# Third attention of a fused four-layer kernel: the row maxima of two heads in one reduction, with the PSUM banks shared out anew

## The reference, cut to what matters

```
qkv = einsum('bnd,ed->bne', z, W_qkv); q, kk, v = 16 heads of 8 channels each
scores = einsum('bhnd,bhmd->bhnm', q, kk) * scale
A = softmax(scores, axis=-1)            # all 512 x 512 scores of a head, no mask
out = einsum('bhnm,bhmd->bhnd', A, v)
x = x + out
```

## Time and profile before

| | us |
|---|---|
| median of three runs | 2079.42 |
| the profiled execution's own time | 2071.99 |
| its span (first to last instruction) | 2070.1 |
| TensorE busy | 1803.5 (87%) |
| VectorE busy | 1292.1 (62%) |
| ScalarE busy | 1042.6 (50%) |
| mean granted TensorE clock | 0.937 |

### The profile page before, as it was taken

The page is one execution under the profiler, slowest core; times in us unless marked ns, Lnnn a source line. Parts: engine busy times, 40 slices in busy tenths (PEclk is TensorE's granted clock), DMA queues, the critical chain, the costliest instruction groups (busy, mean ns, idle before and its releaser), DMA issues.

```text
span 2070.1 us, 33125 instructions
## 1 busy us (share of the span) xinstructions
PE 1803.5 (87%) x11885; PEld 811.1 (39%) x11885; DVE 1292.1 (62%) x3442; ACT 1042.6 (50%) x1768; POOL 713.1 (34%) x796
## 2 busy tenths in 40 slices
PE   4888888656559999998999999999999957999998
PEld 1233333234424444444445443233333234444443
DVE  3777777367767777771111114999999537766663
ACT  1566666412116666663223221888888834454432
POOL 4476776535442223201011012222223036444420
PEclk9899999768869999998999998999999969999999
DMA  5453222000024322400000010333222010000000
GB/s 132 114 139 80 62 67 58 1 17 1 0 61 107 80 63 64 113 11 3 0 0 1 0 49 13 85 88 76 63 63 62 2 51 1 6 6 6 6 11 11
DMA packets 67963, 91.68 MB, mean 44 GB/s; under 512 B 10924, under 2 KB 61340, under 8 KB 62924
## 3 DMA queue, kind: packets, MB, share of 16 engines
q1 hardware_dynamic: 66072, 89.04, 18.1%
q10 hardware_dynamic: 1728, 0.53, 0.2%
HBM read 49.30 MB, written 39.85 MB: 43 GB/s over the span
## 4 chain that ended last, share of the span: by engine, by line
PE 52%; issue 5%; DVE 3%; ACT 3%; DMA 2%; SPq 1%; POOL 1%; DVEq 0%; ACTq 0%; POOLq 0%
PE ps L1442 5%; PE ps L412 5%; PE ps L1454 5%; PE ps L386 4%; PE ps L2885 3%; PE ps L1419 3%; PE ps L2155 3%; PE ps L398 3%; PE ps L2157 2%; PE ps L2173 2%; PE ps L370 2%; PE ps L332 2%; DMA Qst<-mT 2%; PE ps L354 1%; PE ps L1848 1%
## 5 line engine op out<-in xcount | busy, mean ns | idle before, releaser
L702 DVE TENSOR_REDUCE mx<-ps 128x1 f32<-128x512 f32 (+3 forms) x1024 | 534.1, 582 | 108.3 <-PE ps L354 80.0
L600 ACT ACTIVATE Pr<-ps 128x1024 f32<-128x1024 f32 (+3 forms) x512 | 348.0, 706 | 179.3 <-PE ps L337 92.3
L593 ACT ACTIVATE Pr<-ps 128x512 f32<-128x512 f32 x512 | 275.3, 601 | 44.2 <-PE ps L386 37.4
L354 PE MATMUL ps<-Kst,Qst 63*128 63x512 bf16 (+3 forms) x1024 | 221.9, 315 | 55.2 <-DVE mx L702 29.4
L698 DVE CUSTOM_DVE_ANT_0 vs<-ps,cT 128x512 f32<-128x512 f32 (+3 forms) x512 | 225.8, 488 | 61.5 <-PE ps L354 58.0
L332 PE MATMUL ps<-Qst,Kst 64*128 64x512 bf16 (+3 forms) x1024 | 221.8, 310 | 16.9 <-ACT Pr L600 8.4
L2913 POOL TENSOR_TENSOR ve<-mv,eps 128x4 f32<-128x4 f32 x41 | 8.8, 215 | 577.3 <-DVE mv L2902 577.3
L370 PE MATMUL ps<-Pr,V 128*32 128x512 f32 (+3 forms) x2048 | 198.3, 460 | 6.4 <-ACT ctxU L606 2.9
L398 PE MATMUL ps<-Kst,Qst 63*128 63x512 bf16 x512 | 172.7, 404 | 5.5 <-DVE mx L702 3.3
L412 PE MATMUL ps<-Pr,V 128*32 128x256 f32 x2048 | 164.5, 393 | 8.5 <-ACT ctxU L606 7.6
L386 PE MATMUL ps<-Qst,Kst 64*128 64x512 bf16 x512 | 157.6, 388 | 9.7 <-DMA Qst<-mT 5.7
(11 more groups left out here) (340 smaller groups left out, 3272.1 us busy)
## 6 DMA issues: line engine op xcount, KB each, us to landing
Qst<-parts_scratch SPq DMA_DIRECT2D x48, 384.0 KB, 6.4
Kst<-parts_scratch SPq DMA_DIRECT2D x48, 384.0 KB, 8.4
parts_scratch<-qpart SPq DMA_DIRECT2D x24, 384.0 KB, 2.7
parts_scratch<-kpart SPq DMA_DIRECT2D x24, 384.0 KB, 3.2
parts_scratch<-qpart SPq DMA_DIRECT2D x24, 256.0 KB, 2.9
parts_scratch<-kpart SPq DMA_DIRECT2D x24, 256.0 KB, 3.3
parts_scratch<-qpart SPq DMA_DIRECT2D x24, 128.0 KB, 2.8
parts_scratch<-kpart SPq DMA_DIRECT2D x24, 128.0 KB, 3.3
```

The lines of the kernel that those rows point to most:

```text
L354: mm = pe.matmul(ps[:, 4 + a, lo:lo + W], k.Qst[rows, n.par, pair, P * it:P * it + P], k.Kst[rows, n.par, pair, 0:W], start=True, stop=True)
L593: act.activation(k.Pr[:, g % 2, 2 * (j // 2) + 1 - j % 2, :], ps[:, self.bank_t(b, g, j), :], ACT.Exp).then_inc(self.s_exp.sem, 1)
L600: act.activation(k.Pr[:, g % 2, 2 * tile:2 * tile + 2, 0:W], ps[:, 2 * tile:2 * tile + 2, 0:W], ACT.Exp).then_inc(self.s_exp.sem, 1)
L702: dve.tensor_reduce(k.mx[:, half, at:at + 1], ps[:, bank, lo:lo + W], AX_X, ALU.max, negate=True).then_inc(self.s_max.sem, 1)
```

## The change

Row scores get four banks (2 to 5) in two pairs, transposed scores two banks (0 and 1). The two M tiles of a pair of heads go into two neighbouring banks, and one reduction on VectorE over 128 x 2 x 512 takes both maxima. On TensorE the order becomes T0 M0 M1 T1 PV T2 M2 M3 T3 PV. T now waits for the exponential two tiles back, M for the pair two pairs back.

```diff
     def bank_t(self, b, g, j):
-        return (64 * b.c + 4 * g + j) % 3
-
-    def bank_m(self, n, u):
-        return 3 + (64 * n.c + u) % 3
+        return j % 2
+
+    def banks_m(self, u):
+        return 2 + 2 * (u // 2 % 2)
@@ head_t
-            pe.wait_ge(self.s_exp.sem, self.s_exp.at(b, 4 * g + j - 2))
+            pe.wait_ge(self.s_exp.sem, self.s_exp.at(b, 4 * g + j - 1))
@@ head_m
-            pe.wait_ge(self.s_max.sem, self.s_max.at(n, u - 2))
-            pe.matmul(ps[:, self.bank_m(n, u), :], k.Qst[rows, n.par, pair, P * it:P * it + P],
+            pe.wait_ge(self.s_max.sem, self.s_max.at(n, u - a - 2))
+            pe.matmul(ps[:, self.banks_m(u) + a, :], k.Qst[rows, n.par, pair, P * it:P * it + P],
@@ frame of TensorE
-                        if mb.valid():
+                        if mb.valid() and j in (0, 2):
                             head_m(mb, c, j)
+                            head_m(mb, c, j + 1)
@@ maxima
+            if self.kind == "full":
+                for _, u, (it,) in fills[0::2]:
+                    dve.wait_ge(self.s_scores.sem, self.s_scores.at(n, u + 2))
+                    if u % 32 == 0:
+
+                        dve.wait_ge(self.s_mT_ps.sem, self.s_mT_ps.at(n.plus(-1), half + 1))
+                    at = self.banks_m(u)
+                    dve.tensor_reduce(k.mx[:, half, :].rearrange("p (a r) -> p a r", a=2)[:, :, 4 * i + it],
+                                      ps[:, at:at + 2, :], AX_X, ALU.max, negate=True).then_inc(self.s_max.sem, 2)
+                return
```

More of the change, by code:

```diff
@@ L693, in maxima @@
                     at = 16 * a + 4 * i + it
-                    bank = self.bank_m(n, u) if self.kind == "full" else 4 + a
+                    bank = 4 + a
                     if self.kind == "alibi":
```

## The result

The changed kernel takes 2096.41 us in the median of four runs (2094.38 to 2098.70), the kernel before 2077.31 us in runs beside it. The ratio is 1.0098, 95% interval 1.0082 to 1.0113: slower by 0.98%, which is 19 to 20 us. The forecast was 2096 us, in a range of 2080 to 2108.

What follows compares the result with a forecast made beforehand. TensorE was taken to set the pace, busy 43 to 44 us per frame. 7.5 frames x (2.8 - 0.7) = 15.8, -1.1 at the start and +2.5 at the end, made +17.2 on 2079.4: forecast 2096 us, range 2080 to 2108.

Steps and rivals of the forecast that it cites:

- The step that carried it: In a slot with both tile kinds, T3 waits for T1's exponential: a stall of 0.23 us, slot 2.45 instead of 2.22.
- the pair's length: VectorE's reduction over two banks, 1024 elements instead of 512, was to last 1.22 us.
- pitch: Time between starts of back-to-back pair reductions on VectorE: 1.14 us against 1.20 for two single ones.
- the start: Ten slots of row scores alone at VectorE's pace: twenty pairs take 22.8 us instead of 23.9, -1.1 us.
- the last batch: End of the stage, eight slots with T alone at 2.45 instead of 2.08 us: 3.0 us, taken as 2.5.
- The frame's sum: Per frame of 16 slots, stalls of 2.8 us less VectorE's 0.7 us; a frame should take 47.5 us.
- The charge for the stalls: Per frame, 16 stalls of T3, four hidden in waits for the copy of bank 6: 12 x 0.23 = 2.8 us.
- VectorE's relief: Wide reductions save VectorE 1.9 us per frame, of which TensorE was credited with 0.7 us.
- The ceiling of 1.8 us per frame: Most that VectorE's saving could give TensorE: M's waits in weight load and matmul, (8.9 + 2.1) / 6.
- A hidden stall: Rival: T's stalls fall into existing waits and VectorE's gain counts, -6 to -15 us, say 2070 us; chance 0.10.
- cancelling: Rival: stalls cost 2.8 us a frame, VectorE's relief gives the full 1.8; +9 us, 2088 us; chance 0.15.
- a slow reduction: Rival: a two-bank reduction costs two without overlap, 1.36 us, and VectorE becomes the bound; 2115 us; chance 0.05.

Runs made afterwards that it cites:

- the wait alone: Kernel before with T waiting for the exponential two tiles back instead of three, banks, order and reductions as before: 2099.82 us, ratio 1.0105.
- the short copy of V: Changed kernel with ScalarE's copy of V after slot 10 over 128 of 512 columns in the third attention: 2097.72 us in one execution.
- unpaired: Changed kernel with each pair's maxima taken by two reductions of 512 instead of one of 1024: 2097.83 us, ratio 1.0094 against the kernel before.
- the shorter maxima: Kernel before with maxima over 480 of 512 columns in the third attention: 2072.20 us, ratio 0.9978.
- the best: Kernel before with order T0 M0 M1 T1, the transpose of the maxima left between M2 and M3: 2077.01 us, ratio 0.9996.

## Why the prediction was right, and where it was not

**Right in cause and size.** The step that carried it, T3 waits for the exponential of T1 and starts at T0 + 1.57 instead of 1.34, was met to 0.02 us in the slots where ScalarE is free, and the wait alone reproduces the loss. The other terms with a row of their own were met nearly or wholly: the pair's length (1.22 us forecast, 1.221 measured) and pitch (1.14, 1.133), the start (-1.1, measured -0.84) and the last batch (half a frame at 2.1 plus 2.5, 3.6; measured 3.6). Seven frames at +2.1 make 14.7; measured 15.6. The stage was to get 17.2 us longer and got 18.3. That the total was met to 0.4 us is in part luck: the 17.2 us were added to a median of 2079.42 us, which with one more run became 2077.31.

**The frame's sum came near because its errors offset each other.** It was +2.1 us; measured +2.35 (47.72 - 45.37). The charge for the stalls was 12 x 0.23 = 2.8 us. The wait alone measured 2.5 (47.86 - 45.37). By slots:

- 0, 2, 8, 10 and 12 pay 0.2 as worked out (0.16 to 0.23).
- 9 and 13 hide the stall in the wait for bank 6 (-0.02 and +0.08). In slot 5, the fourth of this kind, there is no such wait to hide in: the waits for the copy are 18 in six frames, three a frame and not four, and slot 5 pays 0.41. Slot 1 gets 0.24 shorter, for VectorE is what is late there, and the stall of slot 0 gives it time.
- 6 and 14 pay nothing: the transpose of the maxima stands between T2 and T3 there and holds T3 until 1.65 us in the kernel before. The prediction had every projection and transpose at the end of a slot. 7 and 15 pay nothing because they end in the wait for the landing row, which the prediction had left to the range.
- 3, 4, 5 and 11 pay 0.40. I had taken the 0.43 us from T0 to the exponential from one slot, in which ScalarE was free; behind a copy it is 0.60, and the short copy of V showed that this is the cause in slot 11.

**VectorE's relief was given to the wrong part of the change.** The 0.7 us per frame that I credited to the wide reduction is worth nothing there (unpaired: every slot the same), and 0.25 us even with three T banks. What gave time back is the fourth M bank: slot 1 fell from 3.79 to 3.24 us. I had called this part free of cost and given it no gain. From it 0.42 us go off again for the transpose behind M3, for which the prediction had no term. The ceiling of 1.8 us per frame from the waits was far too high as a price: 8.9 of its 11.0 us stood at a weight load, where the shorter maxima show that a wait is mostly free: 1.9 us less work gave 0.25.

**What a merge saves, and what a bank is worth.** By an estimate from the Trainium skill's fixed 120 cycles ("VectorE: DVE Perf Modes", the TRN2 errata section) a merge would have saved 0.125 us per pair; measured are 1.196 - 1.133 = 0.063 us, and the measurement decides. The Trainium skill's advice to rotate independent matmul groups through banks ("Perfetto Trace Analysis", Optimizing Tensor Performance, Matmuls) bears on both sides here. This case's traces agree with it: T lost a bank and 2.5 us per frame, M won one and 0.55 us in slot 1.

**The rivals.** A hidden stall is refuted by T3's start; cancelling by the frames; a slow reduction by its pitch. What I said would show in the waits came only in part: T (L386) waits for the exponential at its weight load, 81.8 us in six frames against 58.2 before, but hardly as idle time of PE, for M covers it. VectorE's busy time was to fall to 40 us and fell to 41.3: a reduction that waits for its M is counted in full, where back to back ones overlap. ScalarE's was to stay at 38 us and is 39.1.

**Two readings of the kernel before.** The frame of 47.1 us at a clock of 0.96 was taken as a measure of what a lower clock costs. Most of its excess is the late row of maxima, for which TensorE stood 1.73 us; the changed kernel has a frame of 49.1 of the same kind at a clock of 1.00. And the slots are 118 with both kinds of tile and 10 with transposed tiles alone, not 120 and 8: all 128 slots of row scores run, 10 of them ahead of the first T. The sum doesn't hang on it: the last batch's first eight slots got 1.3 us longer, its other eight 2.3, together the 3.6 above.

**What stays open.** A version with three T banks and four M banks would need a ninth bank; sharing bank 7 with one of them wasn't tried. Nor was the changed kernel with the transpose put back between M2 and M3. None of the kernels here that do all the work is faster than the kernel before; the best is equal to it (0.9996).

## What to carry to other kernels

A merged instruction is paid for in buffers: before counting what it saves, ask which ring gives up the banks, and put that ring's round trip from T0 (0.43 us to the reader, 1.09 for two tiles, 0.05 back, 1.57 together) beside the moment at which the bank is due (1.34); here 0.06 us of VectorE's work saved per pair, 0.13 per slot, stood against a stall of 0.23 us per slot. Take the round trip from the slots where the reader's queue is busy with something else, too, not only from a clean one. Changing one wait by one tile, or shortening one instruction by a quarter, is a cheap way to try a ring's depth before rebuilding it.

## What the runs showed of the hardware

One reduction over two PSUM banks (128 x 2 x 512 f32) lasts 1.221 us, the 0.681 us of one bank plus 512 elements at the even rate of the earlier trace rows (0.681 + 0.540); back to back the pitch is 1.133 us. From the end of an exponential to the start of the T that waits for it are 0.054 to 0.056 us in the kernels where T waits for the exponential two tiles back. Crossing from one bank to the next costs nothing that can be seen. Unexpected was how little of a stall reaches the page: with two matmuls side by side in opposite row halves, a kernel that got 19 us slower shows 19 us more of TensorE busy and the same share of 87%.
